# Second attention of a five-stage kernel: other steps of the batch for the input, projection and output work

## The reference, cut to what matters

```python
x = x + _layernorm(_L1_attn_ref(_layernorm(x, axis=-1), L1_attn_Wqkv, L1_attn_bqkv, L1_attn_Wout, L1_attn_bout), axis=-1)

# inside _L1_attn_ref: 16 sequences of 512 tokens, 16 heads of 8 features
qkv = x @ Wqkv + bqkv
q, k, v = (qkv[0], qkv[1], qkv[2])
q = _apply_rope(q, cos, sin)
k = _apply_rope(k, cos, sin)
scores = jnp.einsum('bhqd,bhkd->bhqk', q, k) * scale
attn = jax.nn.softmax(scores, axis=-1)
out = jnp.einsum('bhqk,bhkd->bhqd', attn, v)
out = out.transpose(0, 2, 1, 3).reshape(b, s, dim)
return out @ Wout + bout
```

## Time and profile before

| | |
|---|---|
| median of 3 runs | 2768.68 us (2757.35 to 2777.84) |
| the profiled execution | 2750.51 us, span 2748.7 us |
| PE, DVE, ACT, POOL busy over the span | 75%, 72%, 56%, 44% |
| second attention in the trace | about 1593 us to 2560 us |
| largest group of all | L1788 DVE, the maxima, 614.9 us for 512 |
| next | L1699 ACT, the exponentials, 558.2 us for 1024 |

### The profile page before, as it was taken

The page is one execution under the profiler, slowest core; times in us unless marked ns, Lnnn a source line. Parts: engine busy times, 40 slices in busy tenths (PEclk is TensorE's granted clock), DMA queues, the critical chain, the costliest instruction groups (busy, mean ns, idle before and its releaser), DMA issues. The chain is left out here.

```text
span 2748.7 us, 73587 instructions
## 1 busy us (share of the span) xinstructions
PE 2061.8 (75%) x26748; PEld 1195.5 (43%) x26748; DVE 1992.3 (72%) x5289; ACT 1552.3 (56%) x2872; POOL 1218.4 (44%) x1067
## 2 busy tenths in 40 slices
PE   5988989888988896411009928888888888888587
PEld 3776767676767675400004402232222322322354
DVE  4676767676777666688407817898888988987698
ACT  5665656565655563100004416787777777877587
POOL 5666666666667562000263357632432343230122
PEclk9999999999999998555559968999999999999799
DMA  4333333333333331000022232221112212220001
GB/s 115 75 79 72 71 77 74 75 80 72 79 76 75 71 73 25 1 0 0 19 64 76 81 70 49 51 41 27 25 32 34 33 26 31 35 32 2 13 23 35
DMA packets 103680, 136.73 MB, mean 50 GB/s; under 512 B 23781, under 2 KB 78981, under 8 KB 103046
## 3 DMA queue, kind: packets, MB, share of 16 engines
q1 hardware_dynamic: 99206, 123.34, 20.7%
q0 software_dynamic: 4096, 8.40, 1.1%
HBM read 26.52 MB, written 12.58 MB: 14 GB/s over the span
## 5 line engine op out<-in xcount | busy, mean ns | idle before, releaser
L1788 DVE TENSOR_REDUCE d_nmax_<-d_s_ 128x2 bf16<-128x1024 f32 x512 | 614.9, 1222 | 128.6 <-PE d_s_ L1950 126.9
L1699 ACT ACTIVATE d_pT_<-d_t_ 128x512 f32<-128x512 f32 x1024 | 558.2, 601 | 170.8 <-PE d_t_ L1962 163.3
L268 POOL TENSOR_TENSOR a_other<-a_other,a_rope 128x512 f32<-128x512 f32 x256 | 323.2, 1284 | 358.0 <-DMA a_other<-a_raw 357.2
L1975 PE MATMUL d_o_<-d_pT_,d_v_ 128*32 128x256 f32 x4096 | 326.3, 403 | 0.2 <-ACT d_pT_ L1699 0.2
L1962 PE MATMUL d_t_<-d_qs_,d_ks_ 49*128 49x512 bf16 x1024 | 207.7, 402 | 86.8 <-ACT d_pT_ L1699 41.6
L336 ACT ACTIVATE a_pT<-a_t 64x384 f32<-64x384 f32 x512 | 248.3, 485 | 19.2 <-PE a_t L588 7.5
L476 DVE RECIPROCAL a_rden<-a_o 128x512 f32<-128x512 f32 x64 | 214.7, 3355 | 49.5 <-PE a_o L601 49.4
L299 ACT COPY a_v<-a_proj 128x512 f32<-128x512 f32 x128 | 74.9, 585 | 278.8 <-PE a_proj L499 278.8
L460 DVE TENSOR_REDUCE a_nmax<-a_s 128x4 bf16<-128x384 f32 x256 | 130.7, 552 | 134.7 <-PE a_s L565 134.3
L1950 PE MATMUL d_s_<-d_ks_,d_qs_ 48*128 48x512 bf16 x1024 | 206.9, 400 | 17.5 <-DVE d_nmax_ L1788 12.1
L1155 ACT ACTIVATE c_hT_<-c_in_,c_beta_,c_gamma_ 128x512 f32<-128x512 f32 x16 | 12.4, 777 | 328.0 <-PE c_in_ L1275 328.0
(11 more groups left out here) (260 smaller groups left out, 4641.6 us busy)
## 6 DMA issues: line engine op xcount, KB each, us to landing
a_other<-a_raw SPq DMA_DIRECT2D x512, 128.0 KB, 2.3
d_qs_<-d_part_ SPq DMA_DIRECT2D x192, 64.0 KB
d_ks_<-d_part_ SPq DMA_DIRECT2D x192, 64.0 KB
a_xpre<-x SPq DMA_DIRECT2D x16, 256.0 KB, 3.8
a_xres<-x SPq DMA_DIRECT2D x16, 256.0 KB, 3.5
c_xs_<-sorted_x SPq DMA_DIRECT2D x16, 256.0 KB, 2.7
c_w_<-e_w SPq DMA_DIRECT2D x16, 256.0 KB, 3.3
sorted_x<-c_xs_ SPq DMA_DIRECT2D x16, 256.0 KB, 2.0
```

The source lines that it names most:

```text
L268: nc.gpsimd.tensor_tensor(other[s % 2][:, side, :], other[s % 2][:, side, :], rope[:, 1, :], ALU.mult).then_inc(rope2_done, 1)
L1699: nc.scalar.activation(pT[kt][pair][:, a, :], t_bank(j, turn)[:], ACT.Exp).then_inc(t_read, 1)
L1788: nc.vector.reduce_max(out, s_bank(unit, e)[:], AX_X, negate=True).then_inc(s_read, 1)
L1975: ins = nc.tensor.matmul(o_ps[HC * i:HC * (i + 1), cols], v[e.k][:, kt, g * GH + i, :], pT[kt][i // 2][:, i % 2, cols], start=(kt, half) = ...
```

## The change

Only constants change. AHEAD, the stack, the shifts, the values and all instructions stay; the steps of the once-a-batch extras move. In steps of the batch in which they run (modulo 32), on VectorE: input statistics 8 and 9 to 4 and 9, input aggregation 11 to 12, input normalisation 14 and 15 to 17 and 19, output statistics 16 and 17 to 23 and 24, output aggregation 19 to 25, output normalisation 24 and 27 to 30 and 31, statistics of the sum 3 and 4 to 22 and 27, its aggregation 10 to 28. On TensorE and ScalarE the turned input goes from 18 to 22 and the projections from 19, 20, 21, 22 to 23, 24, 25, 27. On GpSimd the rotary products follow the projections to 24, 25, 26, 28; the differences go from 25, 27, 29, 30 to 29, 31, 0, 1; the addition from 31 to 0. ScalarE's casts go from 24, 27 to 28, 31 and from 28, 29 to 30, 1.

```diff
-    LAST = 74
-
-    STAT_IN, STAT_IN2, ROOT_IN, NORM_IN, NORM_IN2 = -56, -55, -53, -50, -49
-    FOR_ACT = {"turn_in": -46, "q0": -45, "q1": -44, "q2": -43, "q3": -42, "v": -28, "att": 41, "y": 44}
+    LAST = 92
+
+    STAT_IN, STAT_IN2, ROOT_IN, NORM_IN, NORM_IN2 = -60, -55, -52, -47, -45
+    FOR_ACT = {"turn_in": -42, "q0": -41, "q1": -40, "q2": -39, "q3": -37, "v": -28, "att": 41, "y": 44}
     FOR_DVE = {"out0": 13, "out1": 21, "out2": 29, "out3": 37}
-    ROPE = (-44, -43, -42, -41)
-    FIRST_PART, SECOND_PART = (-40, -37), (-36, -35)
-    REST, THIRD_PART = (-39, -37), (-35, -34)
+    ROPE = (-40, -39, -38, -36)
+    FIRST_PART, SECOND_PART = (-36, -33), (-34, -31)
+    REST, THIRD_PART = (-35, -33), (-32, -31)
     STACK = {-32: (0, 0, (0, 1, 2)), -27: (1, 0, (0, 3, 5)), -25: (0, 1, (3, 4)), -23: (1, 1, (1, 4)),
              -22: (0, 2, (5,)), -21: (1, 2, (2,))}
@@
-    STAT_Y, STAT_Y2, ROOT_Y, NORM_Y, NORM_Y2, ADD_Y = 48, 49, 51, 56, 59, 63
-    STAT_SUM, STAT_SUM2, ROOT_SUM = 67, 68, 74
+    STAT_Y, STAT_Y2, ROOT_Y, NORM_Y, NORM_Y2, ADD_Y = 55, 56, 57, 62, 63, 64
+    STAT_SUM, STAT_SUM2, ROOT_SUM = 86, 91, 92
```

## The result

| | kernel before | changed kernel |
|---|---|---|
| median | 2767.61 us (20 runs, 2755.02 to 2784.49) | 2788.77 us (20 runs, 2774.03 to 2801.25) |
| ratio | | 1.007, 95% interval 1.0053 to 1.0086 |
| profiled execution | 2750.51 us, span 2748.7 | 2801.25 us, span 2799.4 |

The change makes the kernel about 0.7% slower; the medians are 21 us apart. The forecast was 2810 us, 41 above the median it started from: the direction and the range hold, the size is about double.

The account below looks back on a forecast made before the run. The first half was taken as bound by SyncE's transfer queue, the second by three engines near the bound getting out of step. Passages 28 + 8 + 2 and ends 3 made 41 us, 2768.7 to 2810 us; range 2755 to 2835.

Parts of the forecast that it names:

- Where the loop jumps back: Passages between batches with a jump: VectorE's lateness partly outlives the stop, +1.6 us each, 8 us for five.
- terms without a jump: Passages without a jump: +0.8 us in the second half and +2.3 in the next first half, nine times, 28 us.
- SyncE's floor: First half: 22.5 us from shifts for step 8 to step 16, whatever the engines' speed; a later start lengthens it equally.
- meetings with GpSimd: VectorE held by GpSimd's instructions: 0.8 us in step 28 (bounds 0 and 1.3), 0.9 in step 31 (0 and 2.3).
- The second half: Steps 16 to 31: step 29's 1.24 us wait goes, waits near step 21 and in step 30 come; +0.8 us per batch.
- The ends: Before batch 0, in batch 0 and behind the last batch: about 3 us added; the last passage 1.8.
- None of the four: Rivals: waits simply go, 2740 (0.14); pile without meetings, 2786 (0.17); change hidden, 2769 (0.12); meetings at upper bound, 2830 (0.07).
- a pile but no meetings: Rival, chance 0.17: VectorE's surplus work at the batch's end costs 17 us without GpSimd holding it, 2786 us.
- meeting at its upper bound: Step 31: both normalisation instructions blocked by GpSimd, 2.3 us; the rival with both meetings at their bounds, 2830 us, chance 0.07.

Follow-up runs that it names:

- before_again: The kernel before with no edit, run for a second trace: 2773.94 us (1 run).
- before_2: The kernel before with no edit, traced again beside the changed kernel on one chip: 2753.13 us, ratio 1.001.
- again: The changed kernel with no edit, run for a second trace: 2792.23 us (1 run).
- after_2: The changed kernel with no edit, traced again beside the kernel before on one chip: 2769.81 us, ratio 1.0047.
- narrow kernels: Kernel before and changed kernel, each with GpSimd's rotary products, sums and differences cut to 64 of 512 columns: 2765.74 us (0.9966) and 2783.0 us (1.001).
- gather_gap: Changed kernel with GpSimd's row gathers skipped in steps 22 to 31 of batch 0 and made up in batch 1: 2760.9 us, ratio 1.0035.
- sum_back: Changed kernel with only the statistics of the sum put back to steps 3, 4 and 10: 2780.58 us, ratio 1.0071.

## Why the prediction was right in direction and wrong in size

The forecast's terms against the means over three traces of each kernel (before, before_again, before_2; the changed kernel's first trace, again, after_2), in us:

| stretch | before | changed | difference | forecast |
|---|---|---|---|---|
| first half, odd batches 3 to 13 | 26.96 | 29.22 | +2.3 | +2.3 |
| second half, even batches 2 to 12 | 26.77 | 27.27 | +0.5 | +0.8 |
| second half with the jump, 3 to 11 | 30.80 | 30.05 | -0.8 | +0.7 |
| first half behind a jump, 4 to 12 | 26.92 | 25.89 | -1.0 | +0.9 |
| sum of the four | 111.45 | 112.43 | +1.0 | +4.7 |

The loop holds this sum about six times: 28 us forecast, 7 us measured (the means of the loops are 664.0 and 671.5; 1.4 to 14 by trace). **The step that failed is "Where the loop jumps back"**: a passage with a jump was to cost +1.6 us (0.7 and 0.9), 8 us in the sum, and it brings 1.8 us (57.7 us before, 55.9 in the changed kernel; by trace 57.5, 57.7, 57.9 and 57.5, 54.7, 55.6). The terms without a jump were about right, +2.8 for +3.1.

With 1.5 us in batches 0 and 1 and 2.6 us behind step 0 of batch 14, the loop's 7 make 11 to 12 us, where after_2 measured 1.0047, 13 us. The 1.007 of the result is some 8 us more; they probably lie in the first two batches (below).

**SyncE's floor: right.** From the shifts for step 8 to step 16 it is 21.9 to 22.8 us in the odd batches of both kernels but one, and whatever makes the transpose of step 2 late makes the half longer by about as much. The exception is batch 7 of the kernel before (20.6, 23.2 and 23.4 us), which isn't explained. The shifts were forecast at 6.8 us; they are at 7.0 in two traces and 6.1 in one.

**The meetings with GpSimd: right in size, one left out.** `d_ve_` in step 28 1.01 - 0.17 = 0.84 (forecast 0.8), the last pair 1.44 - 0.59 = 0.85 in most of one trace (forecast 0.9) and 1.81 in nearly all of two (bound 2.3). The meeting of step 25, 0.71 - 0.17 = 0.54 us, had no term; what it costs was not measured by itself. The rule of the Trainium skill in SBUF — State Buffer, "Who interferes with whom", which the prediction drew on, agrees with all of them: each held instruction ends together with one of GpSimd's. The recorded starts don't show who came first, since VectorE's first instruction of a pair of 2.40 is held though it is recorded 0.05 us ahead of L1629. The narrow kernels show the cause by taking it away.

**The second half: right in its parts, somewhat too dear.** Step 29 falls from 3.0 to 1.7 us (forecast -1.24), and the 0.6 us of waits in steps 27 and 28 are gone. Step 30 rises from 1.1 to 2.2 (+1.06, forecast about 1.4) and step 31 by 0.27 (forecast 0.3). The 0.9 us before the turn of step 21 show as a wait of 0.84 to 0.89 in only four of ten batches of the first trace. Together +0.5 instead of +0.8. Step 13 falls from 2.4 to 1.7 too, which brought nothing, by the floor.

**The jump: wrong.** The prediction said that "VectorE's jump can begin only behind its last normalisation, so its lateness outlives the stop in part", and gave such a passage +1.6 us. The chain at the jump is another. The jumps (COMPARE_BRANCH) of TensorE's and VectorE's queues in the changed kernel, durations in ns and first and last start:

```profile
L1473 PEldq COMPARE_BRANCH  x6: 83/3647/3877, 1925.8 to 2490.8; - x6
...
L1473 DVEq COMPARE_BRANCH  x6: 55/63/74, 1926.7 to 2491.7; - x6
```

and VectorE's last normalisation of batch 3:

```profile
1928.32 1.43 DVE L1814 TENSOR_SCALAR d_yn_<-d_yb_,d_mv_,d_rstd_ 128x128 f32<-128x128 f32 x2
```

VectorE's queue takes the jump at 1926.7, 1.6 us ahead of the normalisation that it was thought to wait for: the pair had been handed over and was still to be worked on. The next instruction of the queue comes 3.3 us later (3.1 to 3.9 in the jumps of the three traces, once 2.9), and in that time VectorE works off what it has. So VectorE's stop and its late work lie side by side and do not add up. The sixth COMPARE_BRANCH, behind batch 13, isn't taken and lasts 0.08 us on TensorE's queue.

Changed kernel, VectorE from step 31 of batch 5 to step 0 of batch 6:

```profile
2042.03 1.43 DVE L1814 TENSOR_SCALAR d_yn_<-d_yb_,d_mv_,d_rstd_ 128x128 f32<-128x128 f32 x2
2044.27 2.36 DVE L1788 TENSOR_REDUCE d_nmax_<-d_s_ 128x2 bf16<-128x1024 f32 x2 [0.80 <-PE d_s_ L1950]
```

and TensorE's first instruction of batch 6:

```profile
2043.60 0.39 PE L1962 MATMUL d_t_<-d_qs_,d_ks_ 49*128 49x512 bf16 x2 [2.74 <-issue]
```

In the kernel before (before_2) TensorE at the same place:

```profile
1997.16 0.61 PE L1962 MATMUL d_t_<-d_qs_,d_ks_ 49*128 49x512 bf16 x2 [3.24 <-issue]
```

VectorE finishes the blocked pair at 2043.46, while TensorE stands, and still has to wait 0.80 us for TensorE's first score tile. So the late work is done under the stop, which the kernel before spent idle: that is the 3.70 of 3.70 us in the stretches above, against 1.03 of 3.80. In again and after_2, where the pair takes 2.40, it ends 0.9 to 1.4 us behind TensorE's restart, and VectorE goes on without a wait. TensorE's own stop is shorter, 2.5 us instead of 3.2 in the mean of the fifteen jumps, since TensorE too has more handed over when its queue jumps: its last matmuls end 1.4 us behind the start of the COMPARE_BRANCH, before 0.9. Step 31 with the jump takes 3.7 instead of 4.4 us. Behind the shorter stop fewer of steps 0 to 2 run at the lower clock (0.61 instead of 0.39 us a pair): 19 of 45, against 32 of 45 in the kernel before. The transpose of step 2 stands 5.3 us behind step 0 there, before 5.8, where the forecast had it later. That the late work costs nothing under the jump can be read from these rows; that the rest of the gain is TensorE's shorter stop and its clock is likely from them, and no run tests it. The Trainium skill in Runtime: NRT & Kernel Launch, section "Instruction fetch mechanics", says that a taken branch out of the loaded window stalls until the target has been fetched; the stop at every jump agrees (TensorE's taken ones last 3.3 to 3.9 us in the changed kernel).

**Given back by the clock.** TensorE ahead of and behind step 16 of batch 3, before_2:

```profile
1856.41 0.39 PE L1962 MATMUL d_t_<-d_qs_,d_ks_ 49*128 49x512 bf16 x2 [2.48 <-DMA d_qs_<-d_nmaxT_]
1857.74 0.61 PE L1962 MATMUL d_t_<-d_qs_,d_ks_ 49*128 49x512 bf16 x2
```

and in the first trace of the changed kernel, with 3.87 us of waiting, the first six at 0.61 (1896.63 and 1898.61 are shown above). In that trace the stop ahead of step 16 is 3.9 to 4.0 us in all five odd batches that a jump follows, long because TensorE was held up less before it, and batch 3's second half runs at a mean clock of 0.79. The second halves with the jump last 31.3 us against 29.4 in again and after_2, and sixteen of their steps are at the lower clock against four and two. In those two VectorE's longer block (2.40) holds TensorE back in step 2 instead, and the stop ahead of step 16 is down to 1.0 to 2.4 us. So in these three traces the dearer meeting is the cheaper loop. It isn't a rule: gather_gap has the dearer meeting too, and its loop is 676.9 us.

**The ends: half right.** The forecast gave batches 0 and 1 and their passages about 8 us, the last passage and the end about 3. On a chip without stops the start costs 119.5 - 118.0 = 1.5 us. On the two chips with stops, again and the five kernels that keep most of the changed positions and the long GpSimd instructions take 145 to 149 us, the three with the positions of before 134 to 137: some 10 us more. (The narrow kernels don't follow this, 142.3 before and 137.7 changed.) From step 0 of batch 14 to the end of the program it is 306.6 - 304.0 = 2.6 us (means of three).

**The rivals.** None of the four is what happened. The measured time is nearest to "a pile but no meetings" (2786), and that mechanism is wrong: the meetings are there, at their forecast size. The time came out there by luck, because the passages with a jump bring time and the first two batches of the chips with stops take some of it back. The normalisation's meeting at its upper bound happened in two of three traces, without costing the total more.

**What stays open.** What the stops in the first two batches are, with "remote" waits of up to 8.9 us. On two chips all 11 traces have them, on two others none of 6; the record doesn't name the chips of the two traces of the result, of which the changed kernel's has them and the other not. That they are the chip's is therefore likely, and not shown. They lie in code that is written out. The Trainium skill holds in Runtime: NRT & Kernel Launch, section "Instruction fetch mechanics", that fetching is mostly hidden in straight code, and the queues marked "instruction" move the same number of packets in the traces read (232 and 146 or 147), so neither speaks for it. One rival was not tested: GpSimd fetches the rows of later batches (L1592) in batches 0 and 1 only, it works on right through the stops, and "remote" waits come in those two batches and in no later one of the 19 traces, batches 14 and 15 included, which are written out as well. gather_gap moved the fetches but ran on chips without stops, and no run leaves them out.

## What to carry to other kernels

Before a lateness of one engine is summed over a loop, look at what each passage does with it. Here a jump kept VectorE's queue for over 3 us while its handed-over work went on, so the late work cost nothing there, and only the passages without a jump paid. A queue's place in the program is not the engine's place in its work: look at both before the two are added. And price a meeting of VectorE with GpSimd by GpSimd's whole instruction, then ask what is next on the path: here it was a queue of transfers two steps later. Putting four transfers behind the urgent ones brought more (1.0%) than any position of the arithmetic that was tried alone.

## What the runs showed of the hardware that was not expected

- Who is first at a meeting can go either way in one program. VectorE's pair beside two GpSimd instructions took 1.44 us (its first instruction 0.34, its second held) or 2.40 (both held, 1.28 and 1.20). With L1629 recorded 0.04 to 0.06 us behind the pair's start both occur, even in one execution; with 0.07 to 0.14 us (all thirteen pairs of sum_back, and the first one of every changed trace with long GpSimd instructions in step 31) it was always 1.44.
- An engine works on while its queue jumps: VectorE's jump at 1926.7, its pair from 1928.32 to 1929.75.
- The lower level of TensorE's clock (1.2 instead of 2.4 GHz, a pair of L1962 in 0.61 instead of 0.39 us, a step in 1.98 instead of 1.11) follows stops ahead of step 16. Counted over batches 2 to 13 of all 19 traces: after each of the 29 stops over 2.7 us one to six of the next six steps ran at it, after 26 of the 31 stops of 2.0 to 2.7 us, 9 of the 14 of 1.5 to 2.0 us and none of the 50 of 0.5 to 1.5 us. Two to three such steps cost about 2 us on top of the stop (estimate, from 0.87 us a step).
- The first two batches take 109 to 120 us on two chips and 134 to 149 on two others, through stops for which the profile finds no instruction and no transfer of the core. Of the 51 us between the two profiles of the result 33 lie there (114.1 and 146.9).
